# Trainium2, a Fourier tokenizer with transformer blocks: the spectra buffer by mode, the mix's weights asked for three steps ahead, its last store in two parts, and no hint in TensorE's pair loops

## What is computed

```python
h = concat(x, grid) @ P_w + P_b                      # 128 images, 64 x 64, 32 channels
for l in range(4):
    g = rfft2(h)[:16, :16]                           # 256 complex modes for each channel
    m = einsum("modes x channels_in x channels_out", g, spec_w[l])   # the mix
    h = leaky(irfft2(m) + conv3x3(h, conv_w[l]) + conv_b[l])
tokens = leaky(h @ Q1 + q1_b) @ Q2 + q2_b
```

## Time and profile before

| | us |
|---|---|
| three runs | 7569.57, 7572.34, 7587.36 (median 7572.34) |
| the profiled execution | 7572.24 |
| its span | 7570.0 |
| busy: TensorE, VectorE, ScalarE | 6734.3, 4997.2, 2567.0 |

### The profile page before, as it was taken

One profiled execution on the slowest core, in us unless ns is written; L12 is line 12 of the kernel. 1 busy time (PEld: TensorE's weight loads), 2 busy tenths in 40 slices (PEclk: granted clock), 3 DMA queues, 4 the chain that ended last, 5 costly groups with the idle time before them and its releaser, 6 DMA issues. The chain is left out here.

```text
span 7570.0 us, 260619 instructions
## 1 busy us (share of the span) xinstructions
PE 6734.3 (89%) x107382; PEld 4009.6 (53%) x107382; DVE 4997.2 (66%) x7931; ACT 2567.0 (34%) x4418; POOL 64.7 (1%) x47
## 2 busy tenths in 40 slices
PE   4699997999999899999989999758888888888888
PEld 3566666666666666666654444334444444444443
DVE  3499995777777477777657777665545545454554
ACT  1244442333333233333223333233343333433334
POOL 1000000000000000000000000000000000000000
PEclk8799998999999899999989999879999999999999
DMA  6666665444444444444432222200000000000000
GB/s 169 150 127 125 127 125 131 122 125 118 123 124 114 132 121 125 118 123 124 112 102 77 76 77 77 88 6 1 3 1 3 3 1 3 1 3 3 1 3 2
DMA packets 657148, 581.17 MB, mean 77 GB/s; under 512 B 328160, under 2 KB 527968, under 8 KB 649190
## 3 DMA queue, kind: packets, MB, share of 16 engines
q1 hardware_dynamic: 656776, 576.22, 31.0%
HBM read 328.55 MB, written 260.39 MB: 78 GB/s over the span
## 5 line engine op out<-in xcount | busy, mean ns | idle before, releaser
L554 PE MATMUL abank<-inv_basis,mode_tile 128*32 128x128 f32 x32768 | 1013.8, 276 | 84.9 <-DMA mode_tile<-m_img 56.6
L600 PE MATMUL zbank<-rows_in,conv_taps 64*32 64x512 f32 (+1 forms) x18432 | 1057.0, 588 | 6.1 <-issue 4.9
L554 PEld LDWEIGHTS abank<-inv_basis,mode_tile 128*32 128x32 f32 x32768 | 877.3, 111 | 259.8 <-issue 259.8
L961 DVE SCALAR_TENSOR_TENSOR rows_out<-zbank,conv_bias,work 128x1024 f32<-128x1024 f32 x512 | 633.9, 1279 | 524.9 <-PE zbank L609 510.0
L822 ACT ACTIVATE turned<-tbank 128x1024 f32<-128x1024 f32 x400 | 410.4, 1026 | 1560.3 <-PE tbank L623 1560.2
L816 ACT ACTIVATE inv_copy<-abank 128x1024 f32<-128x1024 f32 x512 | 524.4, 1024 | 766.6 <-PE abank L554 766.6
L638 PE MATMUL zbank<-fwd_basis,turned 128*64 128x128 f32 x12288 | 758.1, 276 | 19.4 <-ACT turned L822 14.7
L937 DVE TENSOR_TENSOR work<-inv_copy 128x512 f32<-128x512 f32 x1024 | 654.2, 685 | 155.1 <-ACT inv_copy L816 154.8
L638 PEld LDWEIGHTS zbank<-fwd_basis,turned 128*64 128x64 f32 x12288 | 666.5, 137 | 96.9 <-issue 96.9
L609 PE MATMUL zbank<-rows_in,conv_taps 32*32 32x512 f32 (+1 forms) x18432 | 702.5, 593 | 0.0
L600 PEld LDWEIGHTS zbank<-rows_in,conv_taps 64*32 64x32 f32 x18432 | 347.7, 106 | 578.5 <-issue 562.8
(11 more groups left out here) (367 smaller groups left out, 7103.8 us busy)
## 6 DMA issues: line engine op xcount, KB each, us to landing
h_rows<-rows_out SPq DMA_DIRECT2D x768, 256.0 KB, 4.0
rows_in<-h_rows SPq DMA_DIRECT2D x384, 512.0 KB, 4.9
m_img<-rows_out SPq DMA_DIRECT2D x32, 1024.0 KB, 5.4
mode_tile<-m_img SPq DMA_DIRECT2D x512, 64.0 KB, 2.9
rows_in<-x_slots SPq DMA_DIRECT2D x96, 194.9 KB
rows_out<-x_slots SPq DMA_DIRECT2D x96, 194.9 KB
x_slots<-x_pad SPq DMA_DIRECT2D x4, 3121.5 KB
tokens<-spectra SPq DMA_DIRECT2D x512, 4.0 KB
```

The source lines that it names most:

```text
L554: last = nc.tensor.matmul(ab[32 * p:32 * p + 32, s, 128 * k:128 * k + 128], mode_tile[u][:, k, a, :], inv[:, k, s, 128 * p:128 * p + 128], ...
L600: nc.tensor.matmul(section(zb[32 * p:32 * p + 32, 2 * a + so, :])[:, :, :, out], conv_t[part, dx, so, :], moving(part, p, 0, src), start=( ...
L961: nc.vector.scalar_tensor_tensor(out=rows_out[u][:, half].rearrange("p (s x) -> p s x", s=2), in0=zb[:, 2 * a:2 * a + 2, :], scalar=conv_b ...
```

## The change

1. `g_img` keeps its indices, but the mode becomes the outer index in memory: the 128 images of a mode lie side by side, and the 128 modes of an image lie 512 bytes apart. The copies of lines 836, 902 and 1063 write by this order; the matmuls of line 773 read by it.
2. In a mix, SP asks for the weights of step `a + 3` behind the store of step `a - 1`; in layer 0, those of steps 1 to 3 before the loop.
3. The store of step 7 is two transfers: the first 8 images (a semaphore of its own, `m_head`), then the rest. The loads of pair 0's modes wait for the stores of steps up to 6 and for the first part; what follows them waits for the rest.
4. `looped` gives no hint for any engine.

```diff
-        g_img = spectra[:].rearrange("p (n m) -> p n m", n=IMGS)
+        g_img = spectra[:].rearrange("p (m n) -> p n m", n=IMGS)
...
+        m_head = sem("m_head_stored")
...
-            return nc.Fori(start, end, engines=bass.OrderedEngineSet([eng.engine]),
-                           hint_back_edge=eng.engine == mybir.EngineType.PE)
+            return nc.Fori(start, end, engines=bass.OrderedEngineSet([eng.engine]))
...
-            sp.dma_start(m_img[:, :, a, :], mixed[a % 4].rearrange("p (k x) -> p k x", k=4)).then_inc(m_stored[a % 4], 16)
+            if a == 7:
+                sp.dma_start(m_img[0:8, :, a, :], mixed[a % 4][0:8, :].rearrange("p (k x) -> p k x", k=4)).then_inc(m_head, 16)
+            rest = 8 if a == 7 else 0
+            sp.dma_start(m_img[rest:, :, a, :], mixed[a % 4][rest:, :].rearrange("p (k x) -> p k x", k=4))\
+                .then_inc(m_stored[a % 4], 16)
 
         def sp_mix(sp, l, kind):
 
+            if kind == "first":
+                for a in range(1, 4):
+                    sp_load_weights(sp, l, a)
             for a in range(8):
-                if a >= 4 or (a >= 1 and kind == "first"):
-                    sp_load_weights(sp, l, a)
                 if kind == "first" and a in (1, 2, 3, 4):
                     sp_slot(sp, a - 1)
                 if a >= 1:
                     sp_store_mixed(sp, l, a - 1)
+                if 1 <= a <= 4:
+                    sp_load_weights(sp, l, a + 3)
                 if kind == "first" and a >= 4:
                     sp_late_constants(sp, a - 4)
...
             sp_store_mixed(sp, l, 7)
-            for v in range(4):
+            for v in range(3):
                 sp.wait_ge(m_stored[v], 16 * 2 * (l + 1))
                 sp.wait_ge(zeroed, NZERO)
+            sp.wait_ge(m_stored[3], 16 * (2 * l + 1))
+            sp.wait_ge(zeroed, NZERO)
+            sp.wait_ge(m_head, 16 * l + 16)
+            sp.wait_ge(zeroed, NZERO)
             sp_load_modes(sp, 0, 0)
+            sp.wait_ge(m_stored[3], 16 * 2 * (l + 1))
+            sp.wait_ge(zeroed, NZERO)
...
-                            at = 128 * (32 * g + 4 * i)
-                            last = nc.scalar.activation(spectra[:, at:at + CH], xbank[i % 2][g], ACT.Identity)
+                            at = 32 * g + 4 * i
+                            last = nc.scalar.activation(g_img[:, at:at + 4, :], xbank[i % 2][g].rearrange("p (n m) -> p n m", n=4),
+                                                        ACT.Identity)
...
-                            at = 128 * (32 * g + 4 * i)
-                            last = nc.vector.tensor_copy(spectra[:, at:at + CH], xbank[i % 2][g])
+                            at = 32 * g + 4 * i
+                            last = nc.vector.tensor_copy(g_img[:, at:at + 4, :], xbank[i % 2][g].rearrange("p (n m) -> p n m", n=4))
```

## The result

The changed kernel takes 7647.68 us (median of 4 runs, 7636.89 to 7664.09), the kernel before 7574.56 (4 runs, 7569.57 to 7587.36): ratio 1.0093, 95% interval 1.0076 to 1.0111. That is 0.9% longer. The forecast was 7417, its range 7390 to 7570. The profiled execution took 7645.37 us, span 7643.2.

A forecast was written before the change was run, and what follows sets the result against it. TensorE was taken to bound the pairs of layers 1 and 2, chains of waits the mixes. From 7572.2 us, 99 (mixes of layers 1 to 3) and 56 (layer 0) came off: 7417, range 7390 to 7570.

The forecast's parts named there:

- The strided copies: ScalarE's eight copies a pair, layers 0 to 2: writing words 512 bytes apart costs nothing; bounds 0 to 0.82 us a pair.
- the bound, 0.102: Upper bound per ScalarE copy of 128 words: what a strided read costs, 0.218 - 0.116 = 0.102 us.
- 0.1 to spare: Pairs of layers 1 and 2: the copies end some 0.1 us before TensorE's second convolution half needs them.
- rival A: Strided copies cost what a strided read does: 148 us over layers 0 to 2 and expansion, total 7565; chance 0.20.
- the mix matmuls: Mixes: reading weights side by side takes 0.116 us a matmul, not 0.218; 3.7 us a step at full clock.
- rival B: Mix matmuls get no faster, something other than weight reading holding them at 0.218 us; total 7472; chance 0.07.
- the weights of steps 4 to 7: Mixes: asking three steps ahead removes TensorE's waits of 2.8 to 3.38 us; transfers then set 4.1 us a step.
- the split pays for the crowding: End of mixes, layers 1 to 3: two-part store only offsets crowded transfers; first inverse matmul 9.7 us behind the store.
- Either way SP comes to the first rows of the layer at about 207: Layer 0's mix: SP reaches the rows at about 207, not 263.38 us, gaining 56 us; bounds 45 to 62.
- Rival C: Without the hint, 115 loop jumps stall TensorE 1.9 us each, 218 us in all; total 7635, slower; chance 0.08.
- I take 0: Removing the hint from TensorE's pair loops costs nothing; range end -7.6 us if four loop-end stalls vanish.

The follow-up runs named there:

- groups of 2: Changed kernel with the spectra's modes in groups of 2, an image's two words of a group side by side: 7458.22 us, ratio 0.9832.
- layout alone: Kernel before with only the modes in groups of 2; weights, store and hint as before: 7577.07 us against 7582.54, ratio 0.9992.

## Why the prediction was wrong, point by point

**The sum.** The profiled execution is 228 us above the forecast. 180.0 of it are the pairs, 4.6 the expansion, 25.6 layer 0's mix, 3.9 the other mixes, 17.3 the token stages' spread, and -3.1 layer 3's pairs: 228.3.

**The step that failed** is "The strided copies", and in it the sentence "I take nothing: ScalarE needs 0.28 us for 128 words, so each word has more than twice the time that a weight has". The measured price is 0.126 us a copy. It lies above even the bound, 0.102, which was what the read costs TensorE: a bound taken from another engine's reads was no bound for writes. Behind it stood a second error, the "0.1 to spare" in layers 1 and 2, on which rival A charged 0.72 us of its 0.82 a pair. (The two times that it is taken from, 3011.23 and 3008.74 + 2.71, are 0.22 apart.) There is none: 13 ns more a copy lengthen the pair by 0.11 us. That TensorE's idle time before line 600 was 0 did not say that it had slack; 0.11 us a pair can hide in the busy time of that line. Rival A, which had a chance of 0.20, had the mechanism. Its 148 us should have been 185 (with the expansion, and net of what the missing hint gave at the loop ends), and the outcome was slower, on the far side of the 7565 that it gave.

The Trainium skill ("Advanced Engine Details and Errata", "SBUF Cachelines") has the rule that decides here: lines of 16 bytes, a penalty when each access goes to another line, and at least two hits on a line to absorb the latency. The place that the prediction cites has the two hits as well; I had used only its penalty, and only for reads. The runs agree with the whole of it, for reads and writes: one word to a line 394 and 405 ns, two words 281 and 286, four 268 and 269.

**Right:** the mix matmuls, 0.112 to 0.114 us each for the 0.116 of the forecast (a step of 3.7 to 3.8 us at full clock, 6.6 for step 0; rival B falls); the weights of steps 4 to 7, of whose waits 0.81 us is left; eight steps in 35.7 us (3847.34 to 3883.0) where the forecast had 36. The end, from there to the inverse matmul, is 12.7 us, not 11: SP issues the rows until 3884.97 and only then the first part of the store. That the split pays for the crowding was not quite right: it gives 2.0 us of the 3.3 that the crowding costs, so that the end is 1.4 (groups of 2) to 1.7 us longer than the 10.98 of the earlier trace rows.

**Layer 0's mix.** The step "Either way SP comes to the first rows of the layer at about 207" failed. The prediction does not show how 207 comes out; its own length of transfers, 57 us from 164 on, ends at 221. It took SP's issuing and the transfers as two lengths that run side by side, the first with a fixed price an issue. They are not independent: the long issues lie where the DMA engines are full. The second transfers of the three slots take SP 0.70, 6.88 and 9.75 us (0.69, 0.97 and 0.88 in the kernel before), the four rounds of constants 36.4 us (26.5 before, 22 in the forecast). What the slots take beyond the kernel before and the constants beyond the forecast is some 29 us together; with the 4.6 of the expansion it about makes up the 32.7 by which SP is late at the rows. The weights are late too (asked for at 174.39, 184.11 and 198.22, their sign changes come at 191.72, 205.31 and 221.04), but the steps that wait for them end at 229.03, before SP comes to the rows. The DMA engines were full from 171 to 231 us, at 308 to 346 GB/s and not 378; two of six stretches (last two columns: DMA share, GB/s):

```profile
191.00:201.00 10.00, 5.96 (x32) 5.80 (x32) 2.19 (x3) 1.02 (x1) 0.00 (x0) 0.67 1.02 346
...
211.00:221.00 10.00, 1.66 (x14) 1.47 (x12) 0.00 (x0) 1.02 (x1) 0.00 (x0) 0.67 1.05 308
```

Two slots taken out of the stretch shortened it by 18 us. That shows the slots' part in it; that full queues are what makes an issue long is read from the times alone and not shown by a run of its own.

**The hint.** Rival C falls: without the hint no jump inside the loops of layers 0 to 2 costs anything. But "I take 0" was not it either. The stalls of the earlier trace rows at the loop ends are gone without the hint, and the end of the range that the prediction gave, -7.6 us, was the better value (9.0 by the traces, and some 3 more inside layer 3's loop). It is a small term, below the 23 us that a measurement of the whole can tell.

## What to carry to other kernels

When a layout is turned round, one side's stride becomes the other's. Price the stride on the side that has no spare time first, and give each engine two neighbouring words before giving one of them all. And a zero in the idle column of a busy engine is not slack: ask by how much its supplier is early. Where a stretch of transfers and an in-order issuer is estimated, the two are not independent: here an issue of 0.9 us became one of 9.75 while the DMA engines were full.

## What the runs showed of the hardware that was not expected

- Two words to a line of 16 bytes are enough, in either direction and whether side by side or with a gap, for ScalarE's writes (281 and 286 ns against 268 for 128 words) and for TensorE's weights (mean load 205 ns as side by side, against 312 at 512 bytes and 330 at 16).
- Writes of 512 words by ScalarE and VectorE side by side take 594 and 687 ns; with one word to a line 1391 and 1336, which is 2.7 and 2.6 ns a word.
- One word to a line is slightly dearer near than far: 405 against 394 ns written, 330 against 312 loaded.
- The hint cost a little. At each of the four loop ends TensorE idled 0.66 to 2.74 us with it and not without it. In layer 3's loop, pairs were 15.907 us (before), 15.907 (layout alone) and 15.903 (hint put back) apart with it, 15.855 to 15.862 without it in all runs but one (15.80), some 3 us in all. Nothing here shows why, nor why it does so inside that loop only.
- Issues on SP's queue became long while the DMA engines were full: a 3.1 MB copy's second transfer took 6.88 and 9.75 us to issue, against 0.69 to 0.97 in the kernel before.
